# Turning the last two sequences with a matmul that also scales the heads, squares summed on TensorE, and a new order of VectorE's first expert tile

## The reference, cut to what matters

```
x2 = x + tanh(g_xattn) * mlstm(layernorm(x), ctx, ctx)
    C = (q k^T / 4) * D;  h = (C / (max(|sum C|, floor) + eps)) v      per head
    h = (h - mean) * rsqrt(var(h) + eps) * ln_scale                    per head of 16
y  = x2 + tanh(g_ffn) * moe(layernorm(x2))
    logits = 30 tanh(x w_gate / 30); softmax; the best 2 experts of each token
    moe = sum over the 2: (silu(x w1_e) * (x w3_e)) w2_e * weight_e
```

## Time and profile before

| | before |
|---|---|
| median of 3 runs | 229.01 us (228.41 to 229.22) |
| profiled execution, its own time | 229.9 us |
| span of the profiled execution | 228.2 us |
| PE busy | 200.2 us, 88% |
| VectorE busy | 129.3 us, 57% |
| ScalarE busy | 114.1 us, 50% |
| GpSimd busy | 89.1 us, 39% |
| mean granted TensorE clock | 0.94 of full speed |

### The profile page before, as it was taken

How to read it: one execution, slowest core, us unless ns; L and a number is a source line. 1 busy time by engine, 2 the same in 40 slices (tenths; PEclk the granted TensorE clock), 3 DMA queues, 4 the chain that set the end, 5 groups by cost and what they waited for, 6 DMA issues and landing times.

```text
span 228.2 us, 4230 instructions
## 1 busy us (share of the span) xinstructions
PE 200.2 (88%) x1321; PEld 147.0 (64%) x1322; DVE 129.3 (57%) x309; ACT 114.1 (50%) x231; POOL 89.1 (39%) x96
## 2 busy tenths in 40 slices
PE   8999899898979931769999999999999999999940
PEld 2588544444437731257888888888888888888820
DVE  6897584779899759896777842233232222223210
ACT  2488888898865488344666622332223222232210
POOL 8100343365740000510445654554444555552222
PEclk9999999999997555699999999999999999999996
DMA  3999999901011123110223223433323222333222
GB/s 116 311 370 375 371 374 375 342 21 49 0 49 46 46 69 116 50 47 0 46 50 46 46 49 46 57 56 57 65 46 46 46 46 46 49 57 56 24 23 23
DMA packets 20033, 23.41 MB, mean 103 GB/s; under 512 B 3889, under 2 KB 15153, under 8 KB 20017
## 3 DMA queue, kind: packets, MB, share of 16 engines
q1 hardware_dynamic: 13696, 16.94, 21.5%
q0 software_dynamic: 4464, 6.16, 17.0%
q10 hardware_dynamic: 1856, 0.10, 0.5%
HBM read 17.95 MB, written 5.24 MB: 102 GB/s over the span
## 4 chain that ended last, share of the span: by engine, by line
PE 67%; DMA 10%; DVE 8%; ACT 7%; issue 5%; POOL 1%; DVEq 0%; POOLq 0%; ACTq 0%; SPq 0%
PE bank L1359 24%; PE bank L1376 15%; PE bank L1184 6%; DMA out_dram<-hraw,sidx 5%; PE bank L1368 4%; PE bank L1224 4%; DMA x_sb<-in_x_dram 3%; PE bank L1248 3%; ACT arena L496 2%; PE bank L1341 2%; ACT xn_sb L638 2%; PE bank L1088 2%; PE bank L1200 2%; PE bank L1105 1%; DVE w_sb_r L923 1%
## 5 line engine op out<-in xcount | busy, mean ns | idle before, releaser
L456 POOL DMA_INDIRECT out_dram<-hraw,sidx x23 | 37.6, 1633 | 62.9 <-DVE hraw L1046 55.8
L1359 PE MATMUL bank<-arena_r,xn_sb_r 128*128 x184 | 57.2, 392 | 0.0
L1040 DVE TENSOR_TENSOR x_sb<-x_sb,bank 128x512 f32<-128x512 f32 x23 | 15.8, 688 | 56.5 <-ACT x_sb L655 56.5
L1376 PE MATMUL bank<-w_sb,xn_sb 128*128 x184 | 43.6, 380 | 0.8 <-ACT xn_sb L659 0.8
L1359 PE MATMUL bank<-w_sb_r,xn_sb_r 128*128 x92 | 38.2, 416 | 1.4 <-DVE xn_sb_r L1035 1.2
L1359 PEld LDWEIGHTS bank<-arena_r,xn_sb_r 128*128 128x128 f32 x184 | 34.6, 188 | 7.1
L655 ACT ACTIVATE x_sb<-bank 128x512 f32<-128x512 f32 x23 | 13.7, 597 | 49.8 <-PE bank L1359 49.8
L1376 PEld LDWEIGHTS bank<-w_sb,xn_sb 128*128 128x128 f32 x184 | 33.2, 190 | 4.6 <-issue 1.0
L417 POOL TENSOR_SCALAR_AFFINE_SELECT arena<-arena 128x1024 f32<-128x1024 f32 x16 | 17.6, 1102 | 36.5 <-ACT arena L526 36.5
L659 ACT ACTIVATE xn_sb<-bank 128x512 f32<-128x512 f32 x23 | 13.7, 597 | 26.2 <-PE bank L1368 26.2
L439 POOL DMA_INDIRECT cvT<-xnorm_scratch,gidx x12 | 12.3, 1022 | 30.0 <-DVE gidx L992 26.6
(11 more groups left out here) (210 smaller groups left out, 260.3 us busy)
## 6 DMA issues: line engine op xcount, KB each, us to landing
w_sb<-in_L_ffn_w_dram SPq DMA_DIRECT2D x24, 512.0 KB, 9.5
x_sb<-in_x_dram SPq DMA_DIRECT2D x2, 512.0 KB, 6.7
arena<-in_ctx_dram SPq DMA_DIRECT2D x2, 512.0 KB, 9.2
out_dram<-x_sb SPq DMA_DIRECT2D x8, 128.0 KB, 1.8
xnorm_scratch<-xn_sb SPq DMA_DIRECT2D x8, 128.0 KB, 1.8
out_dram<-hraw,sidx POOLq DMA_INDIRECT x23, 3.9
cvT<-xnorm_scratch,gidx POOLq DMA_INDIRECT x12, 3.0
hraw<-xnorm_scratch,gidx POOLq DMA_INDIRECT x11, 2.9
```

Source lines behind the costliest of these rows:

```text
L456: nc.gpsimd.indirect_dma_start(out=out[:, :], out_offset=bass.IndirectOffsetOnAxis(ap=sidx[:, i:i + 1], axis=0), in_=y_sb[i % 2], in_offse ...
L1359: last = nc.tensor.matmul(ps_scores[p][:, n, :], a, w, start=(k == 0 and j == 0), stop=(k == KC - 1 and j == 2))
L1376: last = nc.tensor.matmul(ps_tr[:, 0:H], hT_sb[p][:, k * P:(k + 1) * P], w2_sb[:, bass.ds(e * W2 + k * H, H)], start=(k == 0), stop=(k == ...
```

## The change

In the last group (sequences 6 and 7) `turn_cv` is no longer four transposes but four f32 matmuls of 68 moving columns with a matrix `to_rows`: it turns the heads and multiplies them by `ln_scale` (with its gain) at once, and passes the normaliser column on unscaled. DVE makes `to_rows` and a small matrix `in_head` after `c_mult(1)`. The squares of this group are taken by ACT from the transposed heads (`square_last`, into slot 0 of `dec`) and summed by PE (`spread_last`, four matmuls with 4 moving columns a sequence): `spread_last(0)` stands between `turn_x2(0)` and cv(15), `spread_last(1)` between `turn_cv(7)` and `turn_x2(1)`. ACT's `square_heads(3)`, DVE's sum over the squares and DVE's multiplication by `ln_scale` fall away for this group; DVE waits for `s_spr`, and `finish(3)` now stands ahead of `aggregate_x2(2)`. Two more warming matmuls stand ahead of `turn_x2(3)`. In the first expert tile DVE's `token_slots` and `slot_weights` go behind `lower_x(1)`. PE's queue of the first tile is as before, and `weight_table` still waits for `s_idx`.

```diff
--- before.py
+++ after.py
@@ -118,6 +118,8 @@
         loneg = sb("loneg", [P, 1])
         sel_r = placed("sel32", [P, 32])[1]
         bmask_r = placed("bmask", [P, B])[1]
+        to_rows = sb("to_rows", [P, 4, 4, DH + 1])
+        in_head = sb("in_head", [P, 4])
         tri_s = sb("tri_s", [P, P], BF16)
         ones_b = sb("ones_b", [P, P], BF16)
         iota_r = sb("iota_r", [P, P])
@@ -192,6 +194,7 @@
         hrflat = hraw.rearrange("p b h v -> p (b h v)")
         v_ps = (ps_h, ps_scores[1][:, 0, :])
         pair_ps = (ps_scores[0][:, 0, :], ps_scores[0][:, 1, :], ps_h, ps_ht)
+        sqT = dec[:, 0].rearrange("p h s -> p (h s)").rearrange("p (i n) -> p i n", i=2)
         half_heads = [range(a * HC, (a + 1) * HC) for a in range(2)]
         xflat = x_sb.rearrange("p b h -> p (b h)")
         nflat = xn_sb.rearrange("p b h -> p (b h)")
@@ -267,6 +270,9 @@
         s_df = sem("differences_done")
         s_ex = sem("decay_exp_done")
         s_sq = sem("heads_squared")
+        s_scl = sem("head_scales_spread")
+        s_sqT = sem("last_heads_squared")
+        s_spr = sem("last_spreads_done")
         s_dm = sem("decay_masked")
         s_vc = sem("v_centered")
         s_vp = sem("v_copied")
@@ -536,8 +542,14 @@
                 act.wait_ge(s_ho, b + 1)
                 if b >= 4:
                     act.wait_ge(s_hn, b // 2 - 1)
-                nc.scalar.activation(hraw[:, b % 4], ps_h.rearrange("p (h v) -> p h v", v=VW)[:, :, 0:DH + 1],
+                v = VW if b < B - 2 else DH + 1
+                nc.scalar.activation(hraw[:, b % 4],
+                                     ps_h[:, 0:NH * v].rearrange("p (h v) -> p h v", v=v)[:, :, 0:DH + 1],
                                      ACT.Copy).then_inc(s_hst, 1)
+
+            def square_last(i):
+                act.wait_ge(s_ots, B - 1 + i)
+                nc.scalar.activation(sqT[:, i, :], cvT[:], ACT.Square).then_inc(s_sqT, 1)
 
             def square_heads(g):
                 act.wait_ge(s_hst, 2 * g + 2)
@@ -602,12 +614,13 @@
                 store_cvT(b)
                 if b >= 2 and b % 2 == 0:
                     square_heads(g)
+                if b >= B - 2:
+                    square_last(b - B + 2)
                 if b + 2 < B:
                     mask_q(b + 2, (2, 3))
                 if 2 * b + 4 < 2 * B:
                     decay(2 * b + 4)
             store_cv(B - 1)
-            square_heads(NG - 1)
 
             def upper_weights(e, k):
 
@@ -884,6 +897,15 @@
                 if n == 1:
                     dve.wait_ge(s_tg, 1)
                     nc.vector.tensor_scalar(lns[:], lns[:], tg[:, 0:1], None, ALU.mult).then_inc(s_par2, 1)
+                    dve.wait_ge(s_par2, 2)
+                    rows = ident.rearrange("p (j v) -> p j v", v=VW)
+                    nc.vector.tensor_reduce(in_head[:], rows[:, :, 0:DH], AX_X, ALU.add).then_inc(s_scl, 1)
+                    nc.vector.tensor_tensor(to_rows[:, :, :, 0:DH],
+                                            lns.rearrange("p (g j d) -> p g j d", g=4, d=DH),
+                                            rows[:, :, 0:DH].unsqueeze(1).to_broadcast([P, 4, 4, DH]),
+                                            ALU.mult).then_inc(s_scl, 1)
+                    nc.vector.tensor_copy(to_rows[:, :, :, DH:], rows[:, :, DH:DH + 1].unsqueeze(1).to_broadcast(
+                        [P, 4, 4, 1])).then_inc(s_scl, 1)
                     dve.wait_ge(s_fl, 2)
                     link(nc.vector.tensor_scalar(floor[:], floor[:], MLSTM_EPS, NORM_CAP, ALU.add, ALU.min))
                 if n >= 4:
@@ -902,14 +924,13 @@
 
             g = NG - 1
             center_heads(g)
-            spread_heads(g)
+            dve.wait_ge(s_spr, 2)
+            nc.vector.scalar_tensor_tensor(out=rs[:, 0, :], in0=ps_scores[0][:, 0, 0:NH2], scalar=1.0 / DH,
+                                           in1=s16[:, 2, :], op0=ALU.mult, op1=ALU.add).then_inc(s_var, 1)
             stats_x2(g - 1)
+            finish(g)
             aggregate_x2(g - 1)
-            link(nc.vector.tensor_tensor(hh[:], hraw[:, 2 * g % 4:2 * g % 4 + 2, :, 0:DH],
-                                         lns.rearrange("p (h d) -> p h d", d=DH).unsqueeze(1).to_broadcast(
-                                             [P, 2, NH, DH]), ALU.mult))
-            finish(g)
-            link(nc.vector.tensor_tensor(hflat, hflat, per_head(rs[:, 1, :]), ALU.mult))
+            link(nc.vector.tensor_tensor(hflat, raw_heads(g), per_head(rs[:, 1, :]), ALU.mult))
             add_x2(g)
             stats_x2(g)
             aggregate_x2(g)
@@ -1047,12 +1068,12 @@
                                         ALU.mult).then_inc(s_ys, 1)
 
             lower_x(0, 0)
-            token_slots()
             select_weights()
             split(1)
-            slot_weights()
             hidden(0, 0)
             lower_x(1, 1)
+            token_slots()
+            slot_weights()
             split(2)
             hidden(1, 1)
             lower_x(2, 0)
@@ -1082,10 +1103,10 @@
 
         @block.tensor
         def _(pe):
-            def warm_up(n):
+            def warm_up(n, at=ps_ht):
 
                 for _ in range(n):
-                    nc.tensor.matmul(ps_ht[:, :], ones_b[:], ones_b[:, :].unsqueeze(1).to_broadcast([P, 4, P]),
+                    nc.tensor.matmul(at[:, :], ones_b[:], ones_b[:, :].unsqueeze(1).to_broadcast([P, 4, P]),
                                      start=True, stop=True)
 
             pe.wait_ge(s_ones, 1)
@@ -1229,9 +1250,27 @@
                 pe.wait_ge(s_ots, b + 1)
                 if b >= 1:
                     pe.wait_ge(s_hst, b)
+                if b == B - 2:
+                    pe.wait_ge(s_scl, 3)
                 for g in range(4):
-                    last = nc.tensor.transpose(ps_h[:, g * P:(g + 1) * P], cvT[:, g * P:(g + 1) * P], ident[:])
+                    part = cvT[:, g * P:(g + 1) * P]
+                    if b < B - 2:
+                        last = nc.tensor.transpose(ps_h[:, g * P:(g + 1) * P], part, ident[:])
+                    else:
+                        last = nc.tensor.matmul(ps_h[:, g * 4 * (DH + 1):(g + 1) * 4 * (DH + 1)], part,
+                                                to_rows[:, g].rearrange("p j v -> p (j v)"), start=True, stop=True)
                 last.then_inc(s_ho, 1)
+
+            def spread_last(i):
+
+                pe.wait_ge(s_sqT, i + 1)
+                if i == 0:
+                    pe.wait_ge(s_cm, 2 * B - 1)
+                for g in range(4):
+                    last = nc.tensor.matmul(ps_scores[0][:, 0, i * NH + 4 * g:i * NH + 4 * g + 4],
+                                            sqT[:, i, g * P:(g + 1) * P], in_head[:], start=True, stop=True)
+                last.then_inc(s_spr, 1)
+
             def turn_x2(g):
                 pe.wait_ge(s_x2, g + 1)
                 if g >= 1:
@@ -1283,16 +1322,19 @@
                 if n == 2 * B - 2:
                     pe.wait_ge(s_ex, 2 * B)
                     turn_x2(0)
+                    spread_last(0)
                 if n == 2 * B - 1:
                     logits(0)
                 if n % 2 == 1:
                     turn_cv(n // 2)
+            spread_last(1)
             turn_x2(1)
             warm_up(4)
             logits(1)
             turn_x2(2)
             warm_up(3)
             logits(2)
+            warm_up(2)
             turn_x2(3)
             warm_up(2)
             logits(3)
```

## The result

The changed kernel is slower by half a percent: the ratio to the kernel before is 1.0052 with a 95% interval of 1.0027 to 1.0078, which is 1.2 us on 228.41. The medians of 16 executions each are 231.03 us (228.60 to 234.18) and 228.41 us (228.00 to 231.19). The forecast was 233.2, so 4.3 us more.

The account below looks back on a forecast made before the run. PE was taken as the bound up to the logits, mostly at half clock. Head-part terms of 3.8 us plus 0.5 us in the first expert tile gave 4.3 on 229.01, 233.3, taken as 233.2 us; range 227.8 to 234.9.

Parts of the forecast that it names:

- The step that failed: PE's stretch from 69.23 us to the last logits at 81.71 us: half clock from 70.95 us, used to price new work.
- later-fall: Router stretch: clock falls one stretch later, at about 74.4 us; 230.9 us in all, chance 0.12.
- held-clock: Router stretch: clock stays at 2.4 GHz up to the logits, which end 1.6 us earlier; 227.9 us, chance 0.17.
- cv(15) later by 0.3: Ahead of cv(15): turn_cv(6) and spread_last(0) add 1.5 us and outgrow PE's 1.11 us wait by about 0.3.
- `turn_cv(7)` +0.75: Behind cv(15): turning by matmul sees the clock fall and takes 1.25 instead of 0.49 us.
- `spread_last(1)` 1.5: Behind cv(15): new matmuls on PE, wholly at half clock, adding 1.5 us.
- `turn_x2(1)` +0.4: Behind cv(15): now wholly behind the clock's fall, 0.95 instead of 0.54 us.
- Two warming matmuls 0.85: Ahead of turn_x2(3): the two added warming matmuls cost PE 0.85 us.
- The cover of x2 of the last group: Ahead of turn_x2(3): guess at about 75.9, x2 at 78.3, PE arriving at 81.9 us, so the delay is covered.
- VectorE at n = 1: Between c_mult(1) and c_mult(2): about 0.75 us of new instructions, covered by 0.5 us before the scores, costing nothing.
- The first expert tile: PE waits at weight_table for token_slots until about 102.5 us; turn_h(0) starts at 103.2 instead of 102.73: +0.5 us.
- The rule on transposes: Both turning places: real matmuls replacing transposes could let full clock engage, speaking for the 227.9 us rival, chance 0.17.

Follow-up runs that it names:

- e14: The changed kernel executed once more, unchanged: 232.86 us, logits scaled at 85.08 us.
- e12: Kernel before plus six unused f32 matmuls between turn_cv(7) and turn_x2(1) and two warming matmuls ahead of turn_x2(3): ratio 1.0147, median 232.77 against 229.15 us.
- e8: Changed kernel with VectorE's old first-tile order and turn_x2(1) ahead of spread_last(1) on PE, against the kernel before: ratio 0.9965, median 228.58 against 229.52 us.
- e3: Kernel before with VectorE's new first-tile order, weight_table behind gate_up(1) and slot_weights behind split(2): ratio 0.9993.
- e5: Kernel before with VectorE's new first-tile order, slot_weights ahead of token_slots, weight_table on another PSUM bank without the s_idx wait: ratio 0.9936, median 228.30 against 229.52 us.
- e2: Kernel before with only VectorE's new order in the first expert tile: ratio 0.9992, median 229.40 against 228.91 us.
- e11: Changed kernel with old first-tile order, transposes and ln_scale product back, only squares by matmul, against the kernel before: ratio 0.9937, median 230.99 against 229.15 us.
- e1: Changed kernel with VectorE's old first-tile order, so the head part alone, against the kernel before: ratio 1.0071, median 231.91 against 228.91 us.
- e7: Head part alone without the two warming matmuls added ahead of turn_x2(3), against the kernel before: ratio 1.0029, median 231.82 against 229.52 us.
- e9: Head part with turn_x2(1) ahead of spread_last(1), and weight_table on another PSUM bank, against the kernel before: ratio 0.9852, median 228.04 against 229.15 us.
- e6: Kernel before with five warming matmuls in PE's wait ahead of cv(15): ratio 0.9983, median 228.89 against 229.52 us.
- e13: Kernel before with five warming matmuls ahead of cv(15), four ahead of turn_x2(3), and weight_table on another bank: ratio 0.9918, median 226.71 against 229.22 us.
- e10: Changed kernel with nine warming matmuls between turn_x(1) and weight_table in the first expert tile, against the kernel before: ratio 0.9952, median 229.19 against 229.15 us.

## Why the prediction was wrong, point by point

*Direction and mechanism.* Slower was right, and so was the reason: PE is the bound from `logits(0)` on, and the work taken off ScalarE and VectorE had been hidden. The second trace of the changed kernel (e14) has the forecast's chain nearly term by term. That its 232.86 us stands beside the forecast 233.2 is in part luck: the forecast added 4.3 us to the median of 229.01, while this pattern cost 3.0 us on the 229.9 us that the kernel before takes with it. The added work alone, on the kernel before (e12), gives the loss without any other part.

*The step that failed* is the one that took the clock of one profiled execution for that of the kernel: "all of it but the first 1.7 us runs at clock 0.50" became a premise of each price of the stretch. In the profiled execution of the changed kernel the clock came back from 75.0 to 81.9 us, and the logits were 1.0 us early instead of 3.8 late. The later-fall and the held-clock rivals had 0.12 and 0.17 of the chances. What happened is neither: the clock fell when forecast and came back. The 16 executions range over 5.6 us, while the forecast gave 0.66 to one pattern; only six of them, 232.7 us and above, are near its time. The median of all, 231.03 us, is 2.6 us above before. With the short stretch of half clock on both sides the change costs 1.5 us, not 4.3.

*The terms of the head part*, forecast against e14: cv(15) later by 0.3, measured 68.69 against 68.60 us, 0.09. `turn_cv(7)` +0.75, measured 0.94 against 0.49, +0.45, since the clock fell only behind it. `spread_last(1)` 1.5, measured 1.54. `turn_x2(1)` +0.4, measured 0.95 against 0.54. Two warming matmuls 0.85, measured 0.87. Their sum is 3.4, the measured delay of the logits 3.3, the forecast 3.8. So even in its own pattern the sum was 0.4 us too high, most of it in `turn_cv(7)` and in the time ahead of cv(15). At full clock `turn_cv` took 0.94 to 1.11 and `spread_last` 0.79 to 0.96, near the 1.0 that the forecast took from the earlier trace rows.

*The cover of x2 of the last group.* Right in kind: the guess stood in ScalarE's queue behind `store_xnT(1)`. The guess was done at 75.37 us in e14 (forecast 75.9), x2 at 77.69 (forecast 78.3), and PE reached `turn_x2(3)` at 81.56 (forecast 81.9). At full clock this line does cost, as e8 shows.

*VectorE at n = 1.* Covered, as forecast. The changed kernel's timeline of VectorE:

```profile
31.20 0.22 DVE L902 TENSOR_REDUCE in_head<-ident 128x4 f32<-128x64 f32 x1
31.33 0.42 DVE L903 TENSOR_TENSOR to_rows<-lns,ident 128x256 f32<-128x256 f32 x1
31.66 0.18 DVE L907 COPY to_rows<-ident 128x16 f32<-128x16 f32 x1
```

They end before GpSimd's mask starts at 31.99 us, none is held, and the scores start at 33.79.

*The first expert tile.* `turn_h(0)` did come later as forecast: 3.20 us behind the end of `gate_up(0)` in e14, where before it was 102.73 less 99.97, 2.76. But `gate_up(1)` did not move: 3.61 against 3.64. PE's timelines, first of the kernel before, then of e14:

```profile
103.61 0.49 PE L1359 MATMUL bank<-w_sb_r,xn_sb_r 128*128 x1 [0.23 <-DVE w_sb_r L923]
```

```profile
106.66 0.63 PE L1410 MATMUL bank<-ident,x_sb 128*128 128x128 f32 x4
107.08 0.50 PE L1401 MATMUL bank<-w_sb_r,xn_sb_r 128*128 x1
```

The working let `gate_up(1)` follow `turn_h(0)` at the old distance of 0.88 us. In the kernel before that distance was not set by `turn_h(0)` alone: `gate_up(1)` started 0.60 us behind the end of `lower_x(1)` at 103.01 us, as it did 0.60 and 0.70 us behind it in e3 and e5. In the new order `lower_x(1)` was long done, and `gate_up(1)` followed `turn_h(0)` after 0.42 us in e14. What fills these 0.6 us, the reading of the expert's number or something else, was not taken apart; the row names an instruction of `split(2)`, for which `gate_up(1)` does not wait in the program. So the term was 0.0 and not 0.5; e2's trace agrees (0.07), its ratio can't tell. In the profiled execution of the changed kernel the tile did cost, 0.6 us up to `gate_up(1)` and 0.9 in it (3.90 instead of 3.01), all of it by the clock that gave way behind the 2.44 us wait. In e2 and e14 PE stood there for 2.43 us and the clock did not fall. The forecast had that only as 1 us at the end of its range.

*The rule on transposes* that was weighed, of the Trainium skill, "TensorE: Matmul & The Clock Gate", Part 4 (PE-mode transpose), that full clock does not engage for transposes made by PE, did not decide here. With real matmuls at both places of the turning the clock still fell at 71.20 us in e14 and 71.62 in the first trace; with the transposes back (e11) it held to 79.94 in the one trace.

*What stays open.* Why the clock holds in some executions of one kernel and not in others, and why the kernels with the head part have so many executions above 230 us (9 of 12 in e1 and e7, 7 of 12 in e11, 4 of 8 in e9) while e3, e5, e6 and e13 have none. Such executions go with a low clock: over all kernels with the changed squares the 36 above 232 us had a mean granted clock of 0.908 to 0.941, the 38 under 229.2 us 0.950 to 0.972. The filling with warming matmuls does not explain it alone, since e3 and e5 have none without it, and the kernel before itself had 8 of 35 beside e6 and none of 17 beside e13. It was not tried on the head part, and whether `spread_last(0)` in the wait is the cause was not taken apart.

## What to carry to other kernels

Where TensorE's clock falls in the critical stretch, take more than one trace before pricing anything in it, and price each term at both levels: the same kernel scaled its logits at 80.8 us in one execution and at 85.1 in another. Filling a wait on TensorE with matmuls that nobody reads is worth a try of its own: it cost nothing in e6 and e13 and moved the fall of the clock, while useful work put into the same wait by the change did so in only four of nine traces. When a producer is moved earlier, read the consumer's queue: a step that waits for something else in front of it (`weight_table` for `s_idx`) eats the gain, and if it is moved behind, it comes out of the wait that hid it; here another PSUM bank took the wait away and left the step where it was.

## What the runs showed of the hardware

A wait of 1.1 us on TensorE ahead of cv(15) went with a granted clock of 0.50 (1.2 GHz) from 70.3 to 71.0 us on in all six traces that have it; with it filled the clock stayed at 1.00 (2.4 GHz) up to 76.82 us (e6) and 80.84 us (e13); with `spread_last(0)` in it the fall came anywhere from 70.53 us (e10) to 83.21 us (e8). A wait of 2.4 us in the first expert tile went with a fall in one of three traces (102.34 us in the changed kernel, none in e2 and e14). Once at half clock, a stretch in which PE was busy 13.97 of 14.00 us, with transposes, logits of 8 moving columns and eleven warming matmuls, did not bring it back in e14, while with the same instructions it came back at 75.03 us in the first trace.

An f32 matmul with 128 weight columns cost 0.20 to 0.28 us at full clock whether it moved 4, 8, 68 or 128 columns: `spread_last` 0.79 to 0.96 for four, `logits` 0.99, `turn_cv` 0.94 to 1.11, and 2.03 for the eight of the earlier trace rows. The upper values hold the modelled end of the last one.

When the logits come early, the chain runs over ScalarE's load of its activation table: 1.28 us behind the inverse root and ahead of the tanh. In the changed kernel's profiled execution the tanh starts at 81.29 us instead of 82.07, so of the 1.0 us by which the logits were early 0.8 are left.

```profile
80.00 1.28 ACT L641
81.29 0.27 ACT lt L645
```
